# Reordering the per-tile work around a mixture-of-experts loop: weight loads ahead of table entries, conversions moved under the gate/up products, down products over six PSUM banks

## The reference

```
logits = LN(x) @ gate_kernel                      # (8192, 32)
w, e   = top_k(softmax(logits), 8); w /= sum(w)
rows of LN(x) sorted by expert                    # 65536 (token, expert) pairs
inter  = silu(rows @ gate_proj[e]) * (rows @ up_proj[e])   # 1024 -> 384
y      = inter @ down_proj[e]                     # 384 -> 1024
out    = x + sum over the 8 experts of w * y
```

## Time and profile before

| | us |
|---|---|
| median of 3 runs (10964.43 to 10981.76) | 10968.42 |
| span of the profiled execution, first to last instruction | 10642.6 |
| span to the first gate/up matmul of the experts stage | 3250.5 |
| first matmul of the last tile (tile 143) | 10566.2 |

### The profile page before, as it was taken

How to read it: one execution, slowest core, us unless ns; L and a number is a source line. 1 busy time by engine, 2 the same in 40 slices (tenths; PEclk the granted TensorE clock), 3 DMA queues, 4 the chain that set the end, 5 groups by cost and what they waited for, 6 DMA issues and landing times.

```text
span 10642.6 us, 158415 instructions
## 1 busy us (share of the span) xinstructions
PE 9460.8 (89%) x44752; PEld 7662.4 (72%) x44753; DVE 6681.0 (63%) x11440; ACT 4640.3 (44%) x7725; POOL 5306.1 (50%) x5979
## 2 busy tenths in 40 slices
PE   7888888888877899988899999889898989899988
PEld 5666666666665777777787777777777778687776
DVE  7888888888874555555555555555555555555555
ACT  6766776767752333333333333333333333333333
POOL 2443443434435555555555555555555555555555
PEclk8999999999998999999999999999999999899999
DMA  1111111111104444444445444544444454544543
GB/s 70 41 33 36 39 39 34 39 36 35 39 31 94 106 101 103 99 99 101 101 102 115 101 100 103 117 97 101 100 104 98 99 117 86 119 97 101 119 105 79
DMA packets 418320, 887.57 MB, mean 83 GB/s; under 512 B 156497, under 2 KB 230225, under 8 KB 417746
## 3 DMA queue, kind: packets, MB, share of 16 engines
q0 software_dynamic: 211456, 608.92, 26.7%
q1 hardware_dynamic: 206418, 273.66, 9.3%
HBM read 1039.57 MB, written 375.92 MB: 133 GB/s over the span
## 4 chain that ended last, share of the span: by engine, by line
PE 50%; DMA 8%; issue 4%; POOL 3%; SPq 2%; ACT 1%; DVE 1%; POOLq 0%; ACTq 0%; DVEq 0%
PE bank L1349 34%; PE bank L1363 15%; DMA gu_raw<-in_L_ffn_up_proj 5%; DMA out_rows<-rows_out,entry_now 2%; POOL out_rows L1197 1%; POOL xg L1175 1%; SPq L1140 1%; ACT rows_out L1245 1%; DMA xg<-xn_rows,gather_row 1%; DVE xT_lo L1280 0%; SPq L1129 0%; DVE rows_out L1310 0%; ACT gu_hi L1227 0%; POOL entry_now L1188 0%; ACT xT_hi L1220 0%
## 5 line engine op out<-in xcount | busy, mean ns | idle before, releaser
L1175 POOL DMA_INDIRECT xg<-xn_rows,gather_row x2336 | 2660.5, 1139 | 1570.0 <-DVE xT L1275 880.5
L1349 PE MATMUL bank<-xT_hi,gu_hi 128*128 128x512 f32 (+2 forms) x6912 | 2612.4, 378 | 118.5 <-DVE xT_lo L1280 114.5
L1349 PE MATMUL bank<-xT_lo,gu_hi 128*128 128x512 f32 (+2 forms) x6912 | 2606.4, 377 | 0.0
L1349 PE MATMUL bank<-xT_hi,gu_lo 128*128 128x512 f32 (+2 forms) x6912 | 2605.2, 377 | 0.0
L1238 ACT ACTIVATE gated<-bank 128x512 f32<-128x512 f32 x432 | 258.4, 598 | 3422.3 <-PE bank L1349 3422.3
L1349 PEld LDWEIGHTS bank<-xT_hi,gu_hi 128*128 128x128 f32 x6912 | 1311.5, 190 | 357.8 <-issue 72.3
L1298 DVE TENSOR_TENSOR h<-bank,gated 128x512 f32<-128x512 f32 x432 | 298.4, 691 | 1909.3 <-ACT gated L1238 1909.3
L1349 PEld LDWEIGHTS bank<-xT_lo,gu_hi 128*128 128x128 f32 x6912 | 1312.0, 190 | 229.9
L1349 PEld LDWEIGHTS bank<-xT_hi,gu_lo 128*128 128x128 f32 x6912 | 1311.0, 190 | 230.8
L1363 PE MATMUL bank<-d_hi,h_hi 128*128 128x512 f32 x3222 | 1296.5, 402 | 147.9 <-ACT rows_out L1245 141.6
L1286 DVE TENSOR_TENSOR gu_lo<-gu_raw,gu_hi 128x2048 fp32r<-128x2048 f32 x435 | 983.0, 2287 | 647.9 <-ACT gu_hi L1227 647.9
(11 more groups left out here) (147 smaller groups left out, 15648.4 us busy)
## 6 DMA issues: line engine op xcount, KB each, us to landing
gu_raw<-in_L_ffn_gate_proj SPq DMA_DIRECT2D x580, 384.0 KB
gu_raw<-in_L_ffn_up_proj SPq DMA_DIRECT2D x580, 384.0 KB
d_raw<-in_L_ffn_down_proj SPq DMA_DIRECT2D x145, 1536.0 KB
xg<-xn_rows,gather_row POOLq DMA_INDIRECT x2336
x_t<-in_x SPq DMA_DIRECT2D x64, 512.0 KB
out_rows<-x SPq DMA_DIRECT2D x64, 512.0 KB, 2.6
xn_rows<-xn SPq DMA_DIRECT2D x64, 512.0 KB
entry_in<-slot_table SPq DMA_DIRECT2D x584, 4.0 KB, 1.6
```

What stands on the lines that cost most here:

```text
L1175: pool.indirect_dma_start(out=xg[:, m, :], out_offset=None, in_=quarter_rows, in_offset=bass.IndirectOffsetOnAxis(ap=gather_row[:, m:m + 1 ...
L1349: last = nc.tensor.matmul(bank[:, 0:cols], w[:, c, n, j * P:(j + 1) * P], v[:, c, 0:cols], start=(c == 0 and w is gu_hi and v is xT_hi), s ...
```

## The change

Loop iteration t on SyncE, GpSimd, ScalarE and VectorE is renumbered so that its last tile does not touch tiles past the end; the work that would be t+1 for the last tile is written out after the loop. Inside an iteration the order changes: SyncE loads gate/up first, then the entries, then down. ScalarE converts all three parts of the down weights at the start, two of three column groups of the next tile's gate/up weights before the third `silu`, and the third after the first `left_rows`; VectorE the same with its half. The down products use banks 6, 7, then 0, 1, then 2, 3, then 6, 7. `tiles_used` becomes `tiles_over`, the number above `LEAST_TILES` = 128, and loops start at 2 or 3.

```diff
+    LEAST_TILES = (T * TOP_K + SLOT_ROWS - 1) // SLOT_ROWS
-        GU_BANK, D_BANK = banks[0:6], banks[6:8]
+        GU_BANK = banks[0:6]
+        D_BANK = (banks[6:8], banks[0:2], banks[2:4], banks[6:8])
+        def used_tiles(eng):
+            return eng.value_load(tiles_over[0:1, 0:1], min_val=0, max_val=MOST_TILES - LEAST_TILES) + LEAST_TILES
+        def tiles_from(eng, first, used, tile):
+            with eng.Fori(first, MOST_TILES) as t:
+                with eng.If(t < used):
+                    tile(t)
...
 # SyncE (load_weights split into load_gate_up and load_down, same waits)
             def tile(t):
-                load_entries(t + 2)
-                load_weights(t + 1)
-                hold(d_loaded, 16 * (t + 2))
+                load_gate_up(t - 1)
+                load_entries(t)
+                load_down(t - 1)
+                hold(d_loaded, 16 * t)
+            used = used_tiles(sp)
             load_entries(0)
-            load_weights(0)
+            load_gate_up(0)
+            load_down(0)
             load_entries(1)
-            all_tiles(sp, tile)
+            tiles_from(sp, 2, used, tile)
+            load_gate_up(used - 1)
+            load_down(used - 1)
+            hold(d_loaded, 16 * used)
...
 # GpSimd (take: entry_now <- entry_next; scatter: the four scatters)
+            def take(t):
+                hold(scattered, 16 * Q * t)
...
+            def tile(t):
+                hold(gathered, 16 * RUNS * t)
+                take(t - 2)
+                keep(t - 1)
+                gather(t)
+                scatter(t - 2)
...
+            tile(2)
+            tiles_from(pool, 3, used, tile)
+            hold(gathered, 16 * RUNS * used)
+            take(used - 2)
+            keep(used - 1)
+            scatter(used - 2)
+            take(used - 1)
+            scatter(used - 1)
+            hold(scattered, 16 * Q * used)
...
 # ScalarE
             def tile(t):
                 for k in range(MC):
-                    down_hi(t, k)
-                    silu(t, k)
-                left_rows(t, 0)
-                gate_up_hi(t + 1, 0)
+                    down_hi(t - 1, k)
+                silu(t - 1, 0)
+                silu(t - 1, 1)
+                gate_up_hi(t, 0)
+                gate_up_hi(t, 1)
+                silu(t - 1, 2)
+                left_rows(t - 1, 0)
+                gate_up_hi(t, 2)
                 for c in range(DC):
-                    x_hi(t + 1, c)
+                    x_hi(t, c)
                     if c in ROWS_AFTER:
-                        left_rows(t, 1 + ROWS_AFTER.index(c))
-                for j in range(1, MC):
-                    gate_up_hi(t + 1, j)
+                        left_rows(t - 1, 1 + ROWS_AFTER.index(c))
...
+            tile(1)
+            tiles_from(act, 2, used, tile)
+            for k in range(MC):
+                down_hi(used - 1, k)
+            for j in range(MC):
+                silu(used - 1, j)
+            for q in range(Q):
+                left_rows(used - 1, q)
...
 # VectorE
             def tile(t):
                 for k in range(MC):
-                    down_lo(t, k)
-                    hidden(t, k)
-                    for c in ((0, 1, 2, 3), (4, 5, 6, 7), ())[k]:
-                        transpose_rows(t + 1, c)
-                right_rows(t, 0)
-                gate_up_lo(t + 1, 0)
+                    down_lo(t - 1, k)
+                hidden(t - 1, 0)
+                for c in range(DC // 2):
+                    transpose_rows(t, c)
+                hidden(t - 1, 1)
+                for c in range(DC // 2, DC):
+                    transpose_rows(t, c)
+                gate_up_lo(t, 0)
+                gate_up_lo(t, 1)
+                hidden(t - 1, 2)
+                right_rows(t - 1, 0)
+                gate_up_lo(t, 2)
                 for c in range(DC):
-                    x_lo(t + 1, c)
+                    x_lo(t, c)
                     if c in ROWS_AFTER:
-                        right_rows(t, 1 + ROWS_AFTER.index(c))
-                for j in range(1, MC):
-                    gate_up_lo(t + 1, j)
+                        right_rows(t - 1, 1 + ROWS_AFTER.index(c))
...
 # TensorE, in gate_up(t, j):
+                if j < 2:
+                    wait(pe, left_ready, Q * (t - 1) + j + 2)
+                    wait(pe, right_ready, Q * (t - 1) + j + 2)
 # and for the down groups, in place of a wait for quarter q-1 before each group:
+            def bank_free(t, q, n):
+                if q == 0:
+                    wait(pe, (left_ready, right_ready)[n], Q * t)
+                elif q == Q - 1:
+                    pe.wait_ge((left_ready, right_ready)[n], Q * t + 1)
```

More of the change, by code:

```diff
@@ L1009, in _ @@
             do(dve.tensor_reduce(ends[:, :], part[:, :, :], AX.X, ALU.add))
-            do(dve.tensor_copy(tiles_used[:, :], ends[:, E - 1:E]))
+            do(dve.tensor_scalar(tiles_over[:, :], ends[:, E - 1:E], -float(LEAST_TILES), None, ALU.add))
             do(dve.tensor_tensor(passed[:, :, :],
@@ L1047, in _, with experts_stage @@
             sp.wait_ge(stored, 32)
-def experts_stage(nc, sb, sem, banks, sched_row, tiles_used, xn_dram, table, gate_proj, up_proj, down_v, out, *,
-                  T, D, DC, M, MC, E, TABLE_PAD, MOST_TILES):
+def experts_stage(nc, sb, sem, banks, sched_row, tiles_over, xn_dram, table, gate_proj, up_proj, down_v, out, *,
+                  T, D, DC, M, MC, E, TABLE_PAD, MOST_TILES, LEAST_TILES):
     Q = SLOT_ROWS // P
@@ L1105, in experts_stage @@
         fence = {n: sem(f"fence2_{n}") for n in ("pool", "sp")}
-        def all_tiles(eng, tile):
-            used = eng.value_load(tiles_used[0:1, 0:1], min_val=1, max_val=MOST_TILES)
-            tile(0)
-            with eng.Fori(1, MOST_TILES) as t:
+        def used_tiles(eng):
+            return eng.value_load(tiles_over[0:1, 0:1], min_val=0, max_val=MOST_TILES - LEAST_TILES) + LEAST_TILES
+        def tiles_from(eng, first, used, tile):
+            with eng.Fori(first, MOST_TILES) as t:
                 with eng.If(t < used):
@@ L1136, in load_weights, with load_gate_up @@
                 only = {} if first else {"cond": sp.value_load(sched_row[0:1, bass.ds(4 * t + 2, 1)], min_val=0, max_val=1)}
+                return e, only
+            def load_gate_up(t):
+                e, only = expert_of(t)
                 wait(sp, gulo_ready, MC * t)
@@ L1142, in load_weights, with load_down @@
                                      ).then_inc(gu_loaded, 16)
+            def load_down(t):
+                e, only = expert_of(t)
                 wait(sp, dlo_ready, MC * t)
@@ L1183, in keep @@
                 hold(entry_taken, t + 1)
-            def tile(t):
+            def take(t):
+                hold(scattered, 16 * Q * t)
                 for k in range(KQ):
@@ L1191, in tile, with scatter @@
                 hold(entry_kept, KQ * (t + 1))
-                keep(t + 1)
-                gather(t + 2)
+            def scatter(t):
                 for q in range(Q):
@@ L1210, in _ @@
             gather(1)
-            hold(gathered, 16 * RUNS * 2)
-            all_tiles(pool, tile)
+            tile(2)
[7 more added lines that the diff above has]
+            hold(scattered, 16 * Q * used)
         @block.scalar
@@ L1244, in left_rows @@
                     wait(act, scattered, 16 * Q * t)
-                act.activation(rows_out[:, q, 0:512], D_BANK[0][:, :], ACT.Copy,
+                act.activation(rows_out[:, q, 0:512], D_BANK[q][0][:, :], ACT.Copy,
                                scale=entry_now[:, q, 1:2].bitcast(F32)).then_inc(left_ready, 1)
@@ L1265, in _ @@
                 gate_up_hi(0, j)
-            all_tiles(act, tile)
+            tile(1)
[6 more added lines that the diff above has]
+                left_rows(used - 1, q)
         @block.vector
@@ L1333, in _ @@
                 gate_up_lo(0, j)
-            all_tiles(dve, tile)
+            tile(1)
+            tiles_from(dve, 2, used, tile)
+            for k in range(MC):
+                down_lo(used - 1, k)
+            for j in range(MC):
+                hidden(used - 1, j)
+            for q in range(Q):
+                right_rows(used - 1, q)
         @block.tensor
@@ L1356, in down @@
                 if ks[0] == 0:
-                    wait(pe, (left_ready, right_ready)[n], Q * t + q)
+                    bank_free(t, q, n)
                 for k in ks:
@@ L1362, in down @@
                     for v, w in ((h_hi, d_hi), (h_hi, d_lo), (h_lo, d_hi)):
-                        last = nc.tensor.matmul(D_BANK[n][:, 0:cols], v[:, k, q * P:(q + 1) * P],
+                        last = nc.tensor.matmul(D_BANK[q][n][:, 0:cols], v[:, k, q * P:(q + 1) * P],
                                                 w[:, k, n * 512:n * 512 + cols],
@@ L1386, in empty_group @@
                 q, n = divmod(g, NH)
-                wait(pe, (left_ready, right_ready)[n], Q * t + q)
```

(8 more changed lines are left out.)

22 lines of the change are left out of this document (12 added, 10 removed).

## The result

The changed kernel takes 10692.9 us (median of 4 runs, 10668.2 to 10728.9) against 10966.4 before: ratio 0.9751, 95% interval 0.9731 to 0.9771. The direction was forecast, the size wasn't: 273 us are gone, not 519, and the time lies outside the range of 10350 to 10600.

What follows compares the result with a forecast made beforehand. TensorE was nearly always busy in steady tiles; the loss stood where experts end, waiting for a late gate/up load. Savings 266 + 128 + 45 + 46 + 33 + 1 = 519 took 10968 to 10449 us, range 10350 to 10600.

Steps and rivals of the forecast that it cites:

- What lies around it (325.8 us between span and median) doesn't change: Base of the sum: 325.8 us outside the profiled span stay the same when the span falls to 10124.
- Part 3: Down products over six banks: no wait for a freed bank, 0.52 us per steady tile, 46 us over 88.
- the nine endings: Nine full tiles that end an expert: no stall, 49.2 us against 54.2, saving 45 us.
- rival B: GpSimd, slowed beside VectorE's conversions, becomes the bound: 11570 us; chance 0.06 slower, 0.05 for losing 80 to 300.
- Part 1: SyncE's gate/up load ahead of entries: issued at -7.8, 31 us earlier, taking 28 us, landing at +20.
- my lower bound: Gate/up load takes 21.6 us as before the change, landing at +13.8.
- The 75 us: Extra gain in 256-row tiles if the load lands near +14; within a better-than-forecast case of 10350 us, chance 0.10.
- the 266: Fifteen 256-row tiles with followers: 88.1 us per pair against 105.8, 17.7 saved each, 266 us.
- my chain of a 256-row tile: Load +20, ScalarE conversions to +23.8, VectorE's to +26.5, third hidden step to +28.4; TensorE idles 8 us.
- Part 2, 384 rows: Seven 384-row tiles with followers, conversions ahead of third silu: 87.7 us against 106.0, saving 128 us.
- Part 4: Last tile: no gathers for a nonexistent tile; last scatter from +32, end at +43, saving 33 us.
- the order of the table: Forecasts: 256-row tiles 266, 384-row 128, full tiles ending an expert 45, steady 46, last tile 33, other 1.

Runs made afterwards that it cites:

- a0_before: The unchanged kernel before, timed and profiled a second time: 10970.2 us, ratio 1.0002, profiled span 10971.2 us.
- e1_two_banks: The changed kernel with all down products in banks 6 and 7 again: 10683.1 us, ratio 0.9755.
- f1_last_row_later: The changed kernel with the last block of rows (ScalarE and VectorE) moved behind all eight x_hi and x_lo: 10442.1 us, ratio 0.9514.
- f2_two_banks_last_row_later: The changed kernel with two banks for down products and the last block of rows behind all x_hi and x_lo: 10549.8 us, ratio 0.9612.
- f3_before_load_order: The kernel before with only SyncE's order changed, gate/up load ahead of entries, entries ahead of down load: 10651.5 us, ratio 0.9708.

## Why the prediction was right in sign and wrong in size

**"What lies around it (325.8 us between span and median) doesn't change"** is the premise that failed first. There is nothing around the span but 1.75 us; the 325.8 was the difference between two executions, in `a0_before` 253 us in attention and 75.6 in the experts. It did no harm to the base of the sum, but every duration came from an execution in which TensorE's signals were never late: the trace read before shows no "remote" wait at `rows_out`.

**Part 3, "tile 49.2, x 88 = 46"** is the term that failed most: it measured -106.6, and the nine endings -9.5 instead of 45. The step 0.64 to 0.23 did go, and 43 of the 79 full tiles that neither end an expert nor follow an ending take under 49.6 us. But 31 of them take over 53, mean 55.7. The prediction named this symptom ("steady tiles above 49.7 with TensorE waiting for `xT_lo`") and gave it to rival B; it is another mechanism. The prediction's sum had no term for the last row: `x_hi` and `x_lo` of chunks 6 and 7 stand behind it, and it took its signal to come as soon as the last down matmul ends. The order of instructions turned late signals into stalls, as the place of the last row shows in both directions. In before last rows were late too, but less so (at most 3.6 us), and the steady tile is 1.2 us longer than in the trace without any (50.91 against 49.73). After takes away what held TensorE at each hand-off of a bank, so the next tile starts before the late row has been read; that this is why the six banks gave nothing is argued from `e1_two_banks`, `f1_last_row_later` and `f2_two_banks_last_row_later`, and fits all three.

**Part 1, the load.** Issue at -7.8: it is at -7.4 in tile 8 of after. Landing at +20: in after it can't be read, since ScalarE comes to it later. In `f1_last_row_later` tile 8 starts at 3912.6, the load is issued at 3905.18 and releases ScalarE at 3925.88, so it took 20.7 us, not 28, and landed at +13.2, near my lower bound of 21.6 and +13.8. I had put four scatters inside it; there GpSimd is still issuing gathers, and its first scatter comes at 3926.18. SyncE, ScalarE, GpSimd, the stretch between, and VectorE's first transposes of that tile:

```profile
3905.18 2.11 SPq L1149 DMA_DIRECT2D gu_raw<-in_L_ffn_gate_proj  x4
```
```profile
3925.88 3.72 ACT L1261 ACTIVATE gu_hi<-gu_raw 128x2048 fp32r<-128x2048 f32 x2 [0.74 <-DMA gu_raw<-in_L_ffn_up_proj]
```
```profile
3926.18 1.61 POOL L1218 DMA_INDIRECT out_rows<-rows_out,entry_now  x1 [0.30 <-issue]
```
```profile
3905.20:3925.90 20.70, 20.70 (x145) 19.41 (x144) 12.31 (x17) 8.16 (x13) 16.71 (x14) 1.00 1.02 224
```
```profile
3927.78 2.49 DVE L1319 STREAM_TRANSPOSE xT<-xg 128x512 f32<-128x512 f32 x4 [6.18 <-DMA xg<-xn_rows,gather_row]
```

The 75 us that I had put on such a landing didn't come. In this tile VectorE's transposes wait 6.18 us for the gathers, a wait that my chain of a 256-row tile didn't have, and the third `h_lo` is ready at +28.0, by luck near the forecast +28.4; over the fifteen 256-row tiles it is at +28.3. In after it is at +29.3, and in its tile 8 at +30.5, for another reason: the last two rows of tile 7 are late (VectorE starts them at 3935.91 and 3941.82), TensorE is idle for 4.8 us in the gate/up products of tile 8, and the second `silu` starts at +19.4, in `f1_last_row_later` at +11.9. So the 266 became 245.5 by errors of opposite sign: a load that was costed 7 us too long, and waits for gathers and late rows that weren't in the sum.

**Part 2, 384 rows (128, measured 90):** the same late row; with it moved the group gives 113.4. **Part 4** (33, measured 33.7): the last scatter is at +31.2, the end at +41.9, forecast +32 and +43.

**Rival B** has its mechanism but not its effect. In tile 8 of after the pair of `gu_lo` runs 3959.40 to 3963.85, and GpSimd's row beside it takes 2.23 us where a later tile's takes 0.27:

```profile
3961.76 2.23 POOL L1188 TENSOR_SCALAR gather_row<-entry_in,quarter_no 128x16 int32<-128x16 int32 x1 [3.36 <-DMA entry_in<-slot_table]
...
3969.59 3.02 POOL L1193 DMA_INDIRECT xg<-xn_rows,gather_row  x1 [0.30 <-issue]
...
5611.73 0.27 POOL L1188 TENSOR_SCALAR gather_row<-entry_in,quarter_no 128x16 int32<-128x16 int32 x1 [3.45 <-DMA entry_in<-slot_table]
```

The row ends at 3963.99, 0.14 us after the pair. The Trainium skill, page "SBUF — State Buffer", section "SBUF: two separate sides", says that a VectorE instruction with two inputs in SBUF and a GpSimd one that reads SBUF lock each other out, for the whole of the one that starts first; the trace agrees in this row. GpSimd is late by it, but a clean tile of after still takes 49.2 us: it isn't the bound there. Once the late row is moved, GpSimd is close to being the bound. GpSimd's time to spare, its wait for the transposes before the gathers, is 1057.0 us in `a0_before`, 418.5 in after, 57.4 in `f1_last_row_later`; from one tile's `gather_row` to the next it takes 48.0 us there (median), and the experts stage takes 6939.8 / 144 = 48.2 a tile. The conversions aren't needed for that: `f3_before_load_order`, in the old order, has 53.4 us to spare and the same 48.0.

With the late row out of the way the sum is what the prediction said: the experts stage of `f1_last_row_later` takes 6939.8 us, 7467.7 - 6939.8 = 527.9 less, against 519. The terms, in the order of the table, are 231.0, 113.4, 28.9, 125.0, 33.1 and -3.5, so the agreement is partly luck: the first three are 66 us short of their forecasts together, and the steady tiles gave 79 more, because before pays more there than its first trace showed (4479.9 against 4376.5).

**What stays open.** Why TensorE's signals come late in bursts, why the first profiled execution had none, and why the load order alone makes them rare and takes 1 us off steady tiles. The late last rows stand at the turn of the loop; DMA traffic, instruction supply and the engine's queue weren't told apart.

## What to carry to other kernels

Compare the profiled span with the timed runs before costing anything: where they differ by more than a few microseconds, the durations are of another execution, and waits that a timed run pays can be absent. Where an engine works through its instructions in program order, put one that waits for the newest signal behind everything due sooner, even when it looks just in time; here moving it behind the last two conversions gave 274 us, and one place the other way cost 74 to 149. Test the parts of a reordering alone: the swap of two loads gave more than the change that contained it, and the conversions without it lost 412 us.

## What the hardware did that I had not expected

The signal of a finished matmul reached ScalarE and VectorE up to 10.8 us after its end, in bursts that free both at once (turn from tile 6 to 7 of after: both at 3886.13, after 5.48 and 9.13 us idle), while TensorE's rows go on at full pace. How often depended on the kernel: 78 of 144 tiles in before, 95 in after, 56 with the last row moved, 12 with the load order alone; each count is of one trace.

The trace's semaphore events show where the lateness arises. `down_done` counts finished down groups. In the trace read before, all 1152 groups have a rise of it within 0.15 us of the end of their last matmul; in `a0_before` 672 have one, in after 703. In 71 of the 73 tiles of after with VectorE idle and the last row late, the row starts under 0.1 us after a rise, and the rise is what comes late. So the waiting engine isn't slow to see it. Ends of matmuls are modelled, so TensorE might itself have been late. At the turn from tile 42 to 43 that is not all: the signal rises at 5642.43, and that of the first 48 gate/up matmuls of tile 43 at 5652.39, 9.96 us later, where 48 at the pace of 0.227 take 10.9. So TensorE had left the down products at least 0.9 us before their signal rose; for the rest of the 6.5 us only the modelled times speak.

```profile
3886.13 2.95 ACT L1267 ACTIVATE d_hi<-d_raw 128x1024 fp32r<-128x1024 f32 x3 [5.48 <-remote]
```
```profile
3886.13 0.75 DVE L1354 TENSOR_SCALAR rows_out<-bank,entry_now 128x512 f32<-128x512 f32 x1 [9.13 <-remote]
```
